# The q, k and v stages of an 8-core attention layer: quantization spread over three engines, softmax bounds gathered per tile

## The reference

```python
def fake_quant(x, scale, zero_point):
    q = jnp.clip(round_ste(x / scale + zero_point), QMIN, QMAX)   # 0..255
    return (q - zero_point) * scale

qkv = lora_linear(hidden_states, w_attn, b_attn, la_attn, lb_attn)
q, k, v = jnp.split(qkv, 3, axis=2)          # 16 heads of 64
k = fake_quant(k, kv_scale, kv_zero_point)
v = fake_quant(v, kv_scale, kv_zero_point)
scores = einsum('bhqd,bhkd->bhqk', q, k) / sqrt(64)   # causal mask, softmax
out = einsum('bhqk,bhkd->bhqd', softmax(scores), v)
return lora_linear(out, w_proj, b_proj, la_proj, lb_proj)
```

## Time and profile before

| | |
|---|---|
| median of 2 runs | 7993.11 us (7981.17 to 8005.05) |
| profiled execution, its own time | 7843.69 us |
| its span, slowest core (core 1 of 8) | 7842.2 us |
| spans of the 8 cores | 7797.3 to 7842.2 us |
| mean granted TensorE clock, core 1 | 0.787 of full speed |
| busy over the span | PE 63%, ACT 28%, DVE 25%, POOL 6% |
| third layer on core 1 | starts near 3.37 ms, ends near 6.49 ms |

### The profile page before, as it was taken

The page is one execution under the profiler, slowest core; times in us unless marked ns, Lnnn a source line. Parts: engine busy times, 40 slices in busy tenths (PEclk is TensorE's granted clock), DMA queues, the critical chain, the costliest instruction groups (busy, mean ns, idle before and its releaser), DMA issues. The chain is left out here.

```text
span 7842.2 us, 67204 instructions; the slowest of 8 cores (7797.3 to 7842.2 us)
## 1 busy us (share of the span) xinstructions
...
## 2 busy tenths in 40 slices
...
DMA packets 87162, 298.77 MB, mean 38 GB/s; under 512 B 10886, under 2 KB 10888, under 8 KB 86827
## 3 DMA queue, kind: packets, MB, share of 16 engines
...
...
## 5 line engine op out<-in xcount | busy, mean ns | idle before, releaser
L1029 PE MATMUL p_psY<-p_wdT,p_h 128*128 128x512 bf16 x3072 | 697.0, 390 | 200.8 <-DVE p_xr L1040 184.2
L974 PE MATMUL p_psG<-p_xnT,p_wgT 128*128 128x512 bf16 x3072 | 751.1, 389 | 23.8 <-ACT p_xnT L961 20.5
L985 PE MATMUL p_psU<-p_xnT,p_wuT 128*128 128x512 bf16 x3072 | 731.0, 381 | 0.0
L1407 PE MATMUL p_psA<-p_q,p_k 64*128 64x512 bf16 x880 | 314.9, 465 | 430.6 <-ACT p_st L204 221.6
L999 DVE SCALAR_TENSOR_TENSOR p_h<-p_psU,p_sil 128x512 bf16<-128x512 f32 x384 | 265.7, 692 | 1154.8 <-PE p_psU L985 1081.6
L994 ACT ACTIVATE p_sil<-p_psG 128x512 bf16<-128x512 f32 x384 | 229.7, 598 | 1041.3 <-PE p_psG L974 1041.1
L1029 PEld LDWEIGHTS p_psY<-p_wdT,p_h 128*128 128x128 bf16 x3072 | 304.6, 100 | 593.2 <-issue 256.8
L1277 PE MATMUL p_psA<-p_xnT,p_wattn 128*128 128x512 bf16 x1024 | 383.0, 542 | 92.9 <-DVE p_fq L1165 92.8
L1459 PE MATMUL p_psOA<-p_ptA,p_v 128*64 128x512 bf16 x640 | 294.1, 460 | 197.6 <-DVE p_ptB L1438 150.6
L974 PEld LDWEIGHTS p_psG<-p_xnT,p_wgT 128*128 128x128 bf16 x3072 | 303.9, 100 | 404.0 <-issue 59.6
L985 PEld LDWEIGHTS p_psU<-p_xnT,p_wuT 128*128 128x128 bf16 x3072 | 302.8, 99 | 370.2 <-issue 15.3
...
## 6 DMA issues: line engine op xcount, KB each, us to landing
...
x_s<-p_xr POOLq DMA_DIRECT2D x128, 256.0 KB, 2.4
...
```

The lines of the kernel that those rows point to most:

```text
L974: tokg = sq.do("tensor", lambda e, hc=hc, dch=dch: e.matmul(psG[:], wgT[:, dch * FFN_H + hc * 128: dch * FFN_H + (hc + 1) * 128], xnT[:, d ...
L985: toku = sq.do("tensor", lambda e, hc=hc, dch=dch: e.matmul(psU[:], wuT[:, dch * FFN_H + hc * 128: dch * FFN_H + (hc + 1) * 128], xnT[:, d ...
L1029: e.matmul(psY[:, sl * TILE:(sl + 1) * TILE], h_fm[:, hc * TILE + i * 128: hc * TILE + (i + 1) * 128], wdT[:, hc * D + half * TILE: hc * D ...
L1407: pair=pair: e.matmul(sap, k_fm[off:off + 64, pair * T + stp * 128: pair * T + stp * 128 + 128], q_fm[off:off + 64, pair * TILE:(pair + 1) ...
```

## The change

It has five parts:

1. In `fq_chain`, L1165 moves from DVE to ACT, and L1170, L1190 and L1194 move from DVE to POOL. L1174, L1179 (ACT) and L1184 (DVE) stay.
2. The softmax bound is no longer finished chunk by chunk. Each q chunk only does the |q| sum and the maximum, into a column of its own of `l1m` (now 2x8). The sum alternates between the second bank of `psA` and `psDB`. One cast, one pair of spreading matmuls (8 columns each) and one multiplication follow per tile, behind the k stage.
3. k chunks use the bank `psOA` instead of the first bank of `psA`; it is still one bank.
4. Writes of v always wait for the readers of v, and attention's last matmul of each step is recorded as such a reader.
5. The token that attention waits for before using v is POOL's newest instead of DVE's.

```diff
-    l1m = s_("l1m", [2, 1], F32)
-    l1mb = s_("l1mb", [2, 1], BF16)
+    l1m = s_("l1m", [2, 8], F32)
+    l1mb = s_("l1mb", [2, 8], BF16)
...
-        ta = sq.do("vector", lambda e, zb_ap=zb_ap: e.tensor_scalar(
-            fq1[:], src_ap, kvri[:], zb_ap, ALU.mult, ALU.add),
-            wait=[src_tok, t_kb] + b1.war(), inc="dv")
+        ta = sq.do("scalar", lambda e, zb_ap=zb_ap: e.activation(
+            fq1[:], src_ap, AF.Identity, scale=kvri[:], bias=zb_ap),
+            wait=[src_tok, t_kb] + b1.war(), inc="sc")
...
-        tb = sq.do("vector", lambda e: e.tensor_scalar(
+        tb = sq.do("gpsimd", lambda e: e.tensor_scalar(
             fq1[:], fq1[:], 0.5, 255.5, ALU.max, ALU.min),
-            wait=[ta], inc="dv")
+            wait=[ta], inc="pl")
...
-        tf = sq.do("vector", lambda e: e.tensor_sub(
-            fqr[:], fqr[:], fqg[:]), wait=[te], inc="dv")
+        tf = sq.do("gpsimd", lambda e: e.tensor_sub(
+            fqr[:], fqr[:], fqg[:]), wait=[te], inc="pl")
...
-        tg = sq.do("vector", lambda e: e.tensor_scalar(
+        tg = sq.do("gpsimd", lambda e: e.tensor_scalar(
             dst_ap, fqr[:], kvz_s[:], kvs_s[:], ALU.subtract, ALU.mult),
-            wait=[tf] + list(dst_war), inc="dv")
+            wait=[tf] + list(dst_war), inc="pl")
...
+                ps_qk = psA if part == "q" else psOA
+                pbk = "psA0" if part == "q" else "psOA"
...
+                    lps = psS[0:2, TILE:2 * TILE] if c % 2 == 0 \
+                        else psDB[0:2, 0:TILE]
+                    lbk = "psA1" if c % 2 == 0 else "psDB"
...
+                    tmx = sq.do("vector", lambda e, c=c, lps=lps:
+                                e.tensor_reduce(
+                                    l1m[:, c:c + 1], lps, AX.X, ALU.max),
+                                wait=[tl1] + (bufs["l1m"].war() if c == 0
+                                              else []), inc="dv")
...
+        tcb = sq.do("vector", lambda e: e.tensor_copy(l1mb[:], l1m[:]),
+                    wait=[sq.cur("dv")] + bufs["l1mb"].war(), inc="dv")
...
+        tb1 = sq.do("tensor", lambda e: e.matmul(
+            psDA[:, 0:8], sel2[:, 0:128], l1mb[0:2, :],
+            start=True, stop=False),
+            wait=[tcb] + bufs["psDA"].war())
...
+        t_negc = sq.do("vector", lambda e: e.tensor_scalar(
+            negc[:, :], psDA[:, 0:16], kbneg[:], None, ALU.mult),
+            wait=[tb2] + bufs["negc"].war(), inc="dv")
...
-                    bufs["v"].war() if (i == 0 and j == 0 and half == 0)
-                    else [])
+                    bufs["v"].war())
...
-        t_v_done = sq.cur("dv")
+        t_v_done = sq.cur("pl")
...
+                        bufs["v"].read(tDN)
```

More of the change, by code:

```diff
@@ L1271, in attn_b_phase @@
         bufs["lm"].wrote(t_lm)
+        q_toks = [None] * 8
+        k_toks = [None] * 8
+        abs_toks = [None] * 8
         for part, base_f in (("q", 0), ("k", D)):
@@ L1275, in attn_b_phase @@
                 f0 = base_f + c * 128
+                ps_qk = psA if part == "q" else psOA
+                pbk = "psA0" if part == "q" else "psOA"
                 for dch in range(8):
[L1277 to L1284, removed]
+                    sq.do("tensor", lambda e, f0=f0, dch=dch, ps_qk=ps_qk:
+                          e.matmul(
+                              ps_qk[:, 0:TILE],
+                              wattn[:, dch * H3 + f0: dch * H3 + f0 + 128],
+                              xnT[:, dch * TILE:(dch + 1) * TILE],
+                              start=(dch == 0), stop=False),
+                          wait=(bufs[pbk].war()) if dch == 0 else ())
+                tokm = sq.do("tensor", lambda e, f0=f0, ps_qk=ps_qk: e.matmul(
+                    ps_qk[:, 0:TILE], lb_sb[:, f0:f0 + 128], lm[:],
                     start=False, stop=True),
                     wait=[t_lm], inc="pe")
-                bufs["psA0"].wrote(tokm)
+                bufs[pbk].wrote(tokm)
                 bufs["xnT"].read(tokm)
@@ L1304, in attn_b_phase @@
                     bufs["fqg"].wrote(ta)
-                    tl1 = sq.do("tensor", lambda e: e.matmul(
-                        psS[0:2, TILE:2 * TILE], C["ones2"][:, :], absq[:],
+                    abs_toks[c] = ta
+                    lps = psS[0:2, TILE:2 * TILE] if c % 2 == 0 \
+                        else psDB[0:2, 0:TILE]
+                    lbk = "psA1" if c % 2 == 0 else "psDB"
+                    tl1 = sq.do("tensor", lambda e, lps=lps: e.matmul(
+                        lps, C["ones2"][:, :], absq[:],
@@ L1314, in attn_b_phase @@
[L1314 to L1324, removed]
@@ L1325, in attn_b_phase @@
-                    tb2 = sq.do("tensor", lambda e: e.matmul(
-                        psDA[:, 1:2], sel2[:, 128:256], l1mb[:],
-                        start=False, stop=True),
-                        inc="pe")
-                    bufs["psDA"].wrote(tb2)
-                    bufs["l1mb"].read(tb2)
-                    tnc = sq.do("vector", lambda e, c=c: e.tensor_scalar(
-                        negc[:, 2 * c:2 * c + 2], psDA[:, 0:2], kbneg[:],
-                        None, ALU.mult),
-                        wait=[tb2] + (bufs["negc"].war() if c == 0 else []),
-                        inc="dv")
@@ L1336, in attn_b_phase @@
-                    bufs["psDA"].read(tnc)
-                    bufs["negc"].wrote_more(tnc)
+                    tmx = sq.do("vector", lambda e, c=c, lps=lps:
[3 more added lines that the diff above has]
+                                              else []), inc="dv")
+                    bufs["l1m"].wrote_more(tmx)
+                    bufs[lbk].read(tmx)
@@ L1338, in attn_b_phase @@
                 else:
-                    tk = fq_chain(psA[:, 0:TILE], tokm, bufs["psA0"],
+                    tk = fq_chain(psOA[:, 0:TILE], tokm, bufs["psOA"],
                                   k_fm[:, c * T + jt0: c * T + jt0 + TILE],
@@ L1343, in attn_b_phase @@
                     bufs["k"].wrote_more(tk)
+                    k_toks[c] = tk
+        tcb = sq.do("vector", lambda e: e.tensor_copy(l1mb[:], l1m[:]),
+                    wait=[sq.cur("dv")] + bufs["l1mb"].war(), inc="dv")
+        bufs["l1mb"].wrote(tcb)
+        bufs["l1m"].read(tcb)
+        tb1 = sq.do("tensor", lambda e: e.matmul(
+            psDA[:, 0:8], sel2[:, 0:128], l1mb[0:2, :],
+            start=True, stop=False),
+            wait=[tcb] + bufs["psDA"].war())
+        tb2 = sq.do("tensor", lambda e: e.matmul(
+            psDA[:, 8:16], sel2[:, 128:256], l1mb[0:2, :],
+            start=False, stop=True),
+            inc="pe")
+        bufs["psDA"].wrote(tb2)
+        bufs["l1mb"].read(tb2)
+        t_negc = sq.do("vector", lambda e: e.tensor_scalar(
+            negc[:, :], psDA[:, 0:16], kbneg[:], None, ALU.mult),
+            wait=[tb2] + bufs["negc"].war(), inc="dv")
+        bufs["psDA"].read(t_negc)
+        bufs["negc"].wrote(t_negc)
         for i in range(NSL):
+            vsl = jt0 // 128 + i
             for half in range(2):
```

13 lines of the change are left out of this document (7 added, 6 removed).

## The result

The changed kernel takes 8149.17 us in the median of 12 runs, and the kernel before, run beside it, 7846.37 us in the median of 10. The ratio, which leaves out runs with a lower clock on one die (nine of the twelve, so the medians stand further apart than it says), is 1.0242 with a 95% interval of 1.0173 to 1.0312. So the changed kernel is slower; whether by more than 2% is open. I had forecast 7959 us, a change of -34 us, with a range up to 8065.

A forecast was written before the change was run, and what follows sets the result against it. Chains of waits, not an engine's load, bound the kernel. q -12.8, k +6.8 and v +2.0 us a tile make -32 for eight, another -2 for the last tile: -34 us, from 7993 to 7959; range 7847 to 8065.

The forecast's parts named there:

- What bounds the kernel: In the q, k and v stages the length of chains of waits counts, not an engine's load; nothing outside is moved.
- The base: Whole kernel: 7844 to 7810 us on the profiled execution, applied to the median of the runs shown, 7993, giving 7959.
- POOL's prices: Chain operations moved to POOL: L1190, with two operands, costs 0.95 us; L1170 and L1194, with one, cost 0.77 each.
- the upper bound of 1.89: POOL operations: the whole 1.89 us of the 128x1024 square, if the width counts for nothing.
- The chain: Quantization chain: 3.24 us to the first comparison, 5.23 between comparisons; k stage 41.3 instead of 34.4, +6.8 us a tile.
- v: v stage: three PE restarts -2.1, two last chains +1.9, statistics 2.2 later in seven of eight tiles; +2.0 us a tile.
- The statistics' delay: End of v stage: the next tile's first square stands behind the last L1194, so DVE starts 2.2 us later.
- q: q stage: each chunk loses the cast wait and two small matmuls, 1.6 us; eight chunks, -12.8 us a tile.
- The rival with the full clock: PE in q stages: all at 2.4 GHz, stage 33.2 instead of 47.2 us, -112 us, 7847; chance 0.19.
- Dear POOL: POOL's queue between comparison and next clamp: each operation costs 1.89 us, +266 in all, to 8225; chance 0.18.
- the signs that I had named: Forecast wrong if: POOL row over 1.2 or under 0.5, q stage under 40, attention or projection changed over a few us.

The follow-up runs named there:

- The experiment on prices: The changed kernel, with POOL's clamp and last scaling in k chunks varied (one step less, half the columns, immediates for pointers); 7982 us, a single run.

## Why the prediction was wrong

*What bounds the kernel.* Chains of waits, not loads: right. No stage outside q, k, v and statistics moved.

*The base.* The forecast time, 7959, was worked out from 7993, the median of two runs; ten runs of the same kernel gave 7846. What can be compared is the change: -34 us forecast, +157 in the profiled executions.

*POOL's prices.* This is the step that failed: "L1170 and L1194 have one: 0.77, the middle between 0.59 and 0.95", and with it the upper bound of 1.89. They cost 1.92 and 2.08, L1190 1.15 instead of 0.95. I had carried DVE's ratio between one and two operands over to POOL. With the prices forecast, a chain was to take 5.23 us; it took 7.86. The experiment on prices shows that POOL charges for arithmetic steps, and the one-operand forms here have two. The Trainium skill ("GPSIMD Engine Reference", "Engine selection") has GpSimd roughly at line rate with one input; no form measured here is near that, even one step over one operand takes 1.49 us where DVE does two in 0.43. For two inputs its figure ("Elementwise - side-by-side cycle accounting") gave an estimated 1.1, and 1.15 was measured.

*The chain.* The formula held: with the measured rows, 0.69+0.15+1.15+0.18+2.08+0.09+1.92+0.15+0.63+0.09+0.63+0.10 = 7.86, and 7.86 is the distance of two comparisons. The k stage by the same formula is 4.41 to the first comparison, 7x7.86 and 1.15 behind the last, 60.6; measured 60.6 on average. It was forecast at 41.3, so +6.8 us a tile became +26.2. L1165 on ACT was mis-sized too, 0.78 for 0.69, but it lies beside POOL's queue and not in the period.

*v.* Forecast +2.0 with the statistics, measured +15.7. The sum took PE's restarts as the pace; at 7.86 a chain eight chains are 63 us, and the banks matter only in the first fill. From PE's first matmul to the first comparison it is 11.5 us, then 7x7.86, then 4.25 to the end of the last L1194: 70.8. The statistics' delay was sized 2.2, and the wait grew by 1.9 to 2.2.

*q.* Forecast -12.8 with the clock left as it was, measured -24.8. The wait went as computed (2.09 to 0.31 between the sum and the next chunk); the clock did the rest. This term was mis-sized by 12 us a tile, which hid more than a third of the 33 us a tile by which k and v went over their forecast. The rival with the full clock, 33.2 us, was the right case (35.1 measured) and had 0.19. The experiment that restored a wait shows it as cause: q went back to 56 us; the one that kept the bound chunk by chunk without the wait had 36. The Trainium skill ("TensorE: Matmul & The Clock Gate", "HAM oscillation - how this bites in real kernels") ties the half clock to long gaps between matmuls. Here gaps of 1.51 and 1.04 us a chunk lowered the stage's clock to between 0.59 and 0.78; with 1.51 alone it was 0.97 to 1.00 in all eight tiles of the changed kernel.

*The rivals.* Dear POOL and the full clock came true together, a case I had not priced: 33.2 us a tile dearer by POOL against 14 more gained in q. Their sum from my own numbers, -34+266-112 = +120 us, is near the +136 of the stages, but partly by luck: k came out 4.0 us a tile under that case, v with the statistics 3.9 over it. Two of the signs that I had named came: POOL rows over 1.2 and a q stage under 40. The range stopped at 8065 because I gave POOL's full upper bound too little weight.

*Parts 4 and 5, and the bank for k.* No cost of theirs was seen. They weren't tried alone.
